# GpSimd takes VectorE's divisions and value rests between the halves of an attention stage, and the output projection is moved ahead of the value products

## The chip, the cores and the metric

One core of one Trainium2 chip runs the whole program. The metric is the device time of one execution in microseconds (us); lower is better. Three executions of the kernel before took 1723.38, 1724.31 and 1725.91 us, median 1724.31.

## The reference, cut to what matters

The program is a tower on x of shape (4, 64, 750): a token mixer that gives h of shape (4, 750, 192), a linear attention, a mixture of 8 experts (two per token), a softmax attention with relative positions, and a mixture of 8 experts (one per token). The change is in the softmax attention alone. Per batch element, with 12 heads of 64:

```python
q, k, v = split(x @ wq), split(x @ wk), split(x @ wv)     # (B, 12, 750, 64), x is the layernorm of h
attn = (einsum("bhid,bhjd->bhij", q, k) + einsum("bhid,ijd->bhij", q, rpk)) * 64 ** -0.5
attn = softmax(attn, axis=-1)
out = einsum("bhij,bhjd->bhid", attn, v) + einsum("bhij,ijd->bhid", attn, rpv)
h = h + (out.transpose(0, 2, 1, 3).reshape(B, N, 768) @ wproj + bproj)
```

rpk and rpv are sums of two table rows, one for the vertical and one for the horizontal distance of two places in a 27-wide grid. All is float32.

## The kernel before

**Tiling.** `window_attention` works through 4 batch elements of two halves each, a half being 6 heads (HG). The 750 tokens are 6 tiles of 125 (CH, P). Products run on fp32r operands that are split into a rounded part and a rest (hi and lo), so that a product is three matmuls: hi by hi, hi by lo and lo by hi. The rest is the full value less the rounded one and has to be formed by some engine.

**Words.** In `words` (L2236, L2453, L2769) a half runs 36 steps, one for each head and key tile: scores on TensorE (L2254), two exponentials on ScalarE (L2500: a_Phi rounded, a_PT full), the rest of the exponential on VectorE (L2803: a_Plo), and the value products on TensorE (L2266 to L2273). Eight steps ahead a row product (L2150) and a VectorE maximum (L2678) give each query's maximum, which is turned into a row (L2157, L2684: a_mrow) and laid by a DMA (L1882) into row 127 of a_qhi, so that the scores come out with it subtracted. GpSimd forms the queries' rests (L1970: a_qlo), two heads ahead, and does nothing else in this stage.

**Between two halves** stand, for the old half, the value tables (`value_tables`: TensorE L2100 and L2112, copied by ScalarE L2415 and added by VectorE L2666 into a_outs) and the division of a_outs by the softmax sums (VectorE L2671, three multiplications by a_rdens' copy in the memory of a_qhi), then the projection out; for the new half the query tables (`query_tables`, L2137 to L2144), whose rows ScalarE (L2427) and VectorE (L2726) copy into a_work, one half of the heads each, and then `boundary`. Every engine runs its own list in the order in which it is written, and they meet by counted semaphores:

- TensorE, `boundary` (L2160): the value products `token_values` (L2176, 6 tiles into the two banks of a_S1), the projection out `project_out` (L2192, 6 tiles into the two banks of a_O, one tile of 192 columns in each), the first eight row products `first_rows` (L2150) and `max_to_row` (L2157). `token_values(c)` waits for the rest of tile c-2, which reads the same bank.
- ScalarE, `boundary` (L2420): copies of the queries (L2388), the table rows (L2427), then by turns a head of a_qhi (L2438) and a tile of a_vhi (L2441). The first head waits for the division, whose divisor lies in a_qhi.
- VectorE, `boundary` (L2686): the table rows (L2726), then `update` (L2723, h plus the projected tile), `values_rest` (L2694, a_vlo from the bank and a_vhi), `first_maxima` (L2678) and `first_row` (L2684), by turns.

The first scores of the new half wait for the row DMA (L2247), for the queries' rest (L2246) and for the seventh maximum; the first value product waits for all six value rests (L2279). There are eight such boundaries: one at the entry (no old half), seven between halves; three of the seven end an iteration of a loop over the batch elements, and the last of these leaves the loop. After the last half the old half is divided and projected with no new one.

## Time and profile before

| | |
|---|---|
| median of 3 runs | 1724.31 us (1723.38 to 1725.91) |
| span of the profiled execution, first to last instruction | 1721.1 us |
| its own time beside the span | not listed; the median of the runs is 3.2 us above this span |
| TensorE busy | 1534.4 us, 89% |
| VectorE busy | 1190.8 us, 69% |
| ScalarE busy | 988.4 us, 57% |
| GpSimd busy | 341.2 us, 20% |
| softmax attention, entry boundary to last projection | about 420 to 1505 us |

Engines are PE (TensorE's matmuls), PEld (its weight loads), DVE (VectorE), ACT (ScalarE), POOL (GpSimd) and SPq (the queue from which SyncE issues DMAs). A matmul on plain float32 (L2137, L2192) is two records in the trace, one on fp32r (L2176, L2150) is one. A matmul's end is modelled and overlaps the next one; the starts of the weight loads give the pace.

### The profile page before, as it was taken

To read this page: it belongs to the slowest core of one execution; us is meant where nothing else is said; L and a number is where in the kernel's file an instruction comes from. 1 tells how busy PE (TensorE), PEld (TensorE's weight loads), DVE (VectorE), ACT (ScalarE), POOL (GpSimd) and SP (SyncE) were. 2 spreads that over 40 slices of the span, in tenths; PEclk is the share of its full clock that TensorE was granted. 3 is DMA by queue.
4 is the path that set the end of the run, shared out by engine and by line. 5 is a ranking of instruction groups with operands and counts; after the bars stand their busy time and mean duration, and the time that the engine had idled before them with its cause. 6 is when DMAs were issued, how large, how long until landed. Compare 5 with 4: busy or idle time off the path is not lost. (4 is left out here: it accounts for less than half of the span.)

```text
span 1721.1 us, 32129 instructions
## 1 busy us (share of the span) xinstructions
PE 1534.4 (89%) x10815; PEld 1409.8 (82%) x10816; DVE 1190.8 (69%) x2245; ACT 988.4 (57%) x1777; POOL 341.2 (20%) x499
## 2 busy tenths in 40 slices
PE   5983999937999999899999999999999999848997
PEld 5762999936898898899898899998989889737996
DVE  4887555549775786786787677678677678575443
ACT  5541222226677578578677667667757757562221
POOL 5131566640000000110100010000000010014443
PEclk9985999968999999999999999999999999958999
DMA  8212111164101101100110110110010111091221
GB/s 266 70 51 80 48 57 57 56 142 120 44 11 38 45 11 39 46 11 19 30 44 11 31 45 20 30 44 20 29 45 10 39 35 51 20 291 49 63 58 29
DMA packets 61936, 94.83 MB, mean 55 GB/s; under 512 B 15644, under 2 KB 46511, under 8 KB 61422
## 3 DMA queue, kind: packets, MB, share of 16 engines
q1 hardware_dynamic: 52606, 72.92, 14.7%
q0 software_dynamic: 9200, 20.21, 4.1%
q8 instruction: 78, 1.28, 0.3%
q14 instruction: 52, 0.43, 0.1%
HBM read 72.58 MB, written 21.06 MB: 54 GB/s over the span
## 5 line engine op out<-in xcount | busy, mean ns | idle before, releaser
L2678 DVE TENSOR_REDUCE a_nmx<-a_M 125x1 f32<-125x752 f32 x256 | 240.7, 940 | 129.7 <-PE a_M L2150 128.8
L2500 ACT ACTIVATE a_Phi<-a_S 125x756 fp32r<-125x756 f32 x288 | 231.0, 802 | 156.2 <-PE a_O L2273 146.5
L2803 DVE TENSOR_TENSOR a_Plo<-a_PT,a_Phi 125x756 fp32r<-125x756 f32 x288 | 280.9, 975 | 52.5 <-ACT a_PT L2500 51.7
L1970 POOL TENSOR_TENSOR a_qlo<-a_work,a_qhi 127x750 fp32r<-127x750 f32 x48 | 79.1, 1656 | 996.0 <-PE a_S L2254 509.3
L2500 ACT ACTIVATE a_PT<-a_S 125x756 f32<-125x756 f32 x288 | 230.0, 799 | 0.0
L2254 PE MATMUL a_S<-a_qhi,a_khi 128*125 128x378 f32 x576 | 155.4, 351 | 12.9 <-issue 6.1
L2266 PE MATMUL a_O<-a_Phi,a_vhi 125*128 125x378 f32 x576 | 150.3, 342 | 1.3 <-ACT a_PT L2500 1.3
L2273 PE MATMUL a_O<-a_Plo,a_vhi 125*128 125x378 f32 x576 | 147.5, 337 | 1.0 <-DVE a_Plo L2803 0.9
L2254 PE MATMUL a_S<-a_qhi,a_klo 128*125 128x378 f32 x576 | 146.9, 336 | 0.0
L2254 PE MATMUL a_S<-a_qlo,a_khi 128*125 128x378 f32 x576 | 146.9, 336 | 0.0
L2269 PE MATMUL a_O<-a_Phi,a_vlo 125*64 125x378 f32 x576 | 146.4, 336 | 0.0
L2150 PE MATMUL a_M<-a_khi,a_qhi 127*125 127x376 f32 x512 | 132.2, 339 | 0.4 <-DVE a_nmx L2678 0.4
L1215 PE MATMUL m_psY<-m_w,m_hidT 128*128 x696 | 130.0, 331 | 2.7 <-DVE m_hidT L1572 2.7
L1215 PEld LDWEIGHTS m_psY<-m_w,m_hidT 128*128 128x128 f32 x696 | 114.4, 190 | 9.5 <-issue 9.5
L2254 PEld LDWEIGHTS a_S<-a_qhi,a_khi 128*125 128x125 f32 x576 | 98.3, 187 | 26.4 <-issue 13.5
L2273 PEld LDWEIGHTS a_O<-a_Plo,a_vhi 125*128 125x128 f32 x576 | 104.1, 189 | 14.4 <-DVE a_Plo L2803 4.3
L1299 ACT ACTIVATE m_xT<-m_psX 128x128 fp32r<-128x128 f32 x85 | 23.6, 277 | 155.8 <-PE m_psX L1139 155.8
L1151 PE MATMUL m_psG<-m_w,m_xT 128*128 x540 | 110.9, 352 | 0.5 <-issue 0.4
L2266 PEld LDWEIGHTS a_O<-a_Phi,a_vhi 125*128 125x128 f32 x576 | 102.0, 190 | 11.1 <-issue 8.1
L2254 PEld LDWEIGHTS a_S<-a_qhi,a_klo 128*125 128x125 f32 x576 | 103.9, 187 | 0.0
L2254 PEld LDWEIGHTS a_S<-a_qlo,a_khi 128*125 128x125 f32 x576 | 103.8, 187 | 0.0
L1151 PEld LDWEIGHTS m_psG<-m_w,m_xT 128*128 128x128 f32 x540 | 93.7, 190 | 5.4 <-issue 3.2
(440 smaller groups left out, 3050.3 us busy)
## 6 DMA issues: line engine op xcount, KB each, us to landing
a_qhi<-a_rdens SPq DMA_DIRECT2D x48, 187.5 KB, 3.4
a_wkv<-a_w4k SPq DMA_DIRECT2D x8, 768.0 KB, 5.1
a_wq<-a_w4q SPq DMA_DIRECT2D x8, 768.0 KB, 6.6
a_wkv<-a_w4v SPq DMA_DIRECT2D x8, 768.0 KB, 5.6
m_w<-in_m_w SPq DMA_DIRECT2D x8, 576.0 KB, 9.3
m_X<-m_xn SPq DMA_DIRECT2D x8, 504.0 KB
m_w<-in_m_w SPq DMA_DIRECT2D x8, 384.0 KB, 6.2
m_w_ahead<-in_m_w SPq DMA_DIRECT2D x8, 384.0 KB, 8.1
```

The source lines that it names most:

```text
L1151: last = nc.tensor.matmul(psG[buf][:, g, 0:half], tokens, w1[0:rows_, bass.ds(e, 1), k, g * half:(g + 1) * half].rearrange("d o f -> d (o ...
L1215: last = nc.tensor.matmul(psY[:, 0:E], hidT[:, k * 128:(k + 1) * 128], w2[:, bass.ds(here, 1), k, :].rearrange("f o e -> f (o e)"), start= ...
L1299: nc.scalar.activation(xT[:, buf, 0, :], psX[:, 0:SLOT], ACT.Copy)
L1970: pool.tensor_tensor(qlo[0:ONE, u % HG % QLO, :], work[0:ONE, u % HG, 0:L], qhi[0:ONE, u % HG, :].bitcast(F32), ALU.subtract).then_inc(sg[ ...
L2150: last = nc.tensor.matmul(bank[0:P, a, 0:376], qhi[0:ONE, u % HG, c * P:(c + 1) * P], khi[0:ONE, u % HG, a * 374:a * 374 + 376], start=Tru ...
L2254: last = nc.tensor.matmul(psS[wd % 2][0:P, a, 0:HP], kk[:, u % HG, at], qq[:, PART[a]:PART[a] + HP], start=(x == 0), stop=(x == 2))
L2266: nc.tensor.matmul(psO[:, a, 0:HP], vhi[:, c, u % HG, :], Phi[:, wd % 2, at[a]], start=(c == 0), stop=False)
L2269: nc.tensor.matmul(psO[0:HD, a, 0:HP], vlo[:, c, u % HG, :], Phi[:, wd % 2, at[a]], start=False, stop=False)
L2273: last = nc.tensor.matmul(psO[:, a, 0:HP], vhi[:, c, u % HG, :], Plo[:, wd % 2, at[a]], start=False, stop=(c == CH - 1))
L2500: last = nc.scalar.activation(to[:, wd % 2, :].rearrange("p (a l) -> p a l", a=2), psS[wd % 2][0:P, :, 0:HP], ACT.Exp, scale=SCALE)
L2678: v.tensor_reduce(nmx[:, u % 2, c:c + 1], bank[0:P, :, 0:376], AX.XY, ALU.max, negate=True).then_inc(sg["max_ready"], 1)
L2803: v.tensor_tensor(Plo[:, wd % 2, :], PT[:, wd % 2, :], Phi[:, wd % 2, :].bitcast(F32), ALU.subtract).then_inc(sg["exp_rest"], 1)
```

## The change

- **Division.** The three multiplications of a boundary between halves go from VectorE to GpSimd, at the same point of the program. After the last half they stay on VectorE.
- **Value rests.** GpSimd forms a_vlo from a full copy of each value tile in SBUF (`vfull`, in the memory of a_pairs, five tiles deep), which ScalarE makes ahead of a_vhi. A bank of a_S1 is free once ScalarE has made both copies; VectorE no longer reads it.
- **Projection out.** Two tiles share a bank of a_O (384 columns), so 6 tiles are 3 groups. Groups 0 and 1 stand ahead of the value products, group 2 after the fourth row product. VectorE adds two tiles of h in one instruction.
- **ScalarE's order.** A head of a_qhi comes before value tiles 0, 2 and 4; heads 3, 4 and 5 come after all value tiles.
- **GpSimd's order.** Its list becomes: division, rest of head 0, value rests 0 and 1, rest of head 1, value rests 2 to 5, and, inside the words, the rests of heads 2 to 5.

```diff
+VF = 5
...
+        vfull = pairs[0:P].rearrange("p a l -> p (a l)")[:, 0:VF * HG * HD].rearrange("p (c e) -> p c e", c=VF)
...
-            "projected": 12,
-            "h_updated": 12,
+            "projected": 6,
+            "h_updated": 6,
...
-            with pool.Fori(0, B) as i:
+
+            def queries_rest(i, u):
+
                 wait = waiter(pool, i)
-                for half in range(2):
-                    for u in range(half * HG, half * HG + HG):
-
-                        wait("qhi_ready", u + 1)
-                        if u % HG >= QLO:
-                            wait("scores_ready", (u - QLO + 1) * CH)
-                        pool.tensor_tensor(qlo[0:ONE, u % HG % QLO, :], work[0:ONE, u % HG, 0:L],
-                                           qhi[0:ONE, u % HG, :].bitcast(F32), ALU.subtract
-                                           ).then_inc(sg["qlo_ready"], 1)
+                wait("qhi_ready", u + 1)
+                if u % HG >= QLO:
+                    wait("scores_ready", (u - QLO + 1) * CH)
+                pool.tensor_tensor(qlo[0:ONE, u % HG % QLO, :], work[0:ONE, u % HG, 0:L],
+                                   qhi[0:ONE, u % HG, :].bitcast(F32), ALU.subtract
+                                   ).then_inc(sg["qlo_ready"], 1)
+
+            def values_rest(i, half, c):
+
+                waiter(pool, i)("vhi_ready", half * CH + c + 1)
+                pool.tensor_tensor(vlo[:, c, :, :], vfull[:, c % VF, :].rearrange("p (h d) -> p h d", d=HD),
+                                   vhi[:, c, :, 0:64].bitcast(F32), ALU.subtract).then_inc(sg["vlo_ready"], 1)
+
+            def divide(i, half):
+
+                waiter(pool, i)("rel_h_added", (half + 1) * (NHS + 1))
+                pool.wait_ge(s_db, (2 * i + half + 1) * (32 * NPR))
+                for pr in range(NPR):
+                    pool.tensor_tensor(outs[:, pr, 0:L], outs[:, pr, 0:L], rdb[:, pr, :], ALU.mult
+                                       ).then_inc(sg["out_divided"], 1)
+
+            def boundary(i, half):
+
+                u0 = half * HG
+                queries_rest(i, u0)
+                values_rest(i, half, 0)
+                values_rest(i, half, 1)
+                queries_rest(i, u0 + 1)
+                for c in range(2, CH):
+                    values_rest(i, half, c)
+
+            def words(i, half):
+
+                for u in range(half * HG + QLO, half * HG + HG):
+                    queries_rest(i, u)
+
+            boundary(0, 0)
+            with pool.Fori(0, B - 1) as i:
+                words(i, 0)
+                divide(i, 0)
+                boundary(i, 1)
+                words(i, 1)
+                divide(i, 1)
+                boundary(i + 1, 0)
+            words(B - 1, 0)
+            divide(B - 1, 0)
+            boundary(B - 1, 1)
+            words(B - 1, 1)
...
                     else:
-                        wait("vlo_ready", half * CH + c - 1)
+                        wait("vhi_ready", half * CH + c - 1)
...
-                def project_out(c):
+                def project_out(g):
 
                     if old is None:
                         return
                     i, half = old
                     wait = waiter(pe, i)
-                    if c == 0:
+                    if g == 0:
                         pe.wait_ge(s_wp, 32 * i + 16 * (half + 1))
                         wait("out_divided", half * NPR + NPR)
-                    if c >= 2:
-                        wait("h_updated", half * CH + c - 1)
-                    for pr in range(NPR):
-                        last = nc.tensor.matmul(psO[0:P, c % 2, 0:E], outs[:, pr, c * P:(c + 1) * P],
-                                                wp[:, pr, :], start=(pr == 0), stop=(pr == NPR - 1))
+                    if g == 2:
+                        wait("h_updated", half * 3 + 1)
+                    for z in range(2):
+                        c = 2 * g + z
+                        for pr in range(NPR):
+                            last = nc.tensor.matmul(psO[0:P, g % 2, z * E:(z + 1) * E], outs[:, pr, c * P:(c + 1) * P],
+                                                    wp[:, pr, :], start=(pr == 0), stop=(pr == NPR - 1))
                     last.then_inc(sg["projected"], 1)
...
+                project_out(0)
+                project_out(1)
                 token_values(0)
                 token_values(1)
-                project_out(0)
-                project_out(1)
                 first_rows(0)
                 first_rows(1)
                 token_values(2)
+                first_rows(2)
+                token_values(3)
+                first_rows(3)
                 project_out(2)
-                first_rows(2)
-                first_rows(3)
-                token_values(3)
-                project_out(3)
                 first_rows(4)
                 first_rows(5)
+                token_values(4)
                 first_rows(6)
-                token_values(4)
-                project_out(4)
+                token_values(5)
                 first_rows(7)
-                token_values(5)
-                project_out(5)
...
-                for x in range(HG):
+                def head(x):
+
                     nc.scalar.activation(qhi[0:ONE, x, :], work[0:ONE, x, 0:L], ACT.Copy
                                          ).then_inc(sg["qhi_ready"], 1)
+
+                def values(x):
+
                     wait("v_product", half * CH + x + 1)
+                    if x >= VF:
+                        wait("vlo_ready", half * CH + x - VF + 1)
+                    nc.scalar.activation(vfull[:, x % VF, :], psS[1][0:P, x % 2, 0:HG * HD], ACT.Copy)
                     nc.scalar.activation(vhi[:, x, :, 0:64],
                                          psS[1][0:P, x % 2, 0:HG * HD].rearrange("p (h d) -> p h d", d=HD),
                                          ACT.Copy).then_inc(sg["vhi_ready"], 1)
+
+                for x in range(HG):
+                    if x % 2 == 0:
+                        head(x // 2)
+                    values(x)
...
+                for x in range(HG // 2, HG):
+                    head(x)
...
-                wait("rel_h_added", (half + 1) * (NHS + 1))
+
+            def divide(i, half):
+
+                waiter(dve, i)("rel_h_added", (half + 1) * (NHS + 1))
                 dve.wait_ge(s_db, (2 * i + half + 1) * (32 * NPR))
                 for pr in range(NPR):
...
-                def values_rest(c):
-
-                    if new is None:
-                        return
-                    i, half = new
-                    waiter(dve, i)("vhi_ready", half * CH + c + 1)
-                    v.tensor_tensor(vlo[:, c, :, :],
-                                    psS[1][0:P, c % 2, 0:HG * HD].rearrange("p (h d) -> p h d", d=HD),
-                                    vhi[:, c, :, 0:64].bitcast(F32), ALU.subtract).then_inc(sg["vlo_ready"], 1)
-
...
-                def update(c):
+                def update(g):
 
                     if old is None:
                         return
                     i, half = old
                     wait = waiter(dve, i)
-                    if c == 0:
+                    if g == 0:
                         dve.wait_ge(s_bp, i + 1)
-                    wait("projected", half * CH + c + 1)
+                    wait("projected", half * 3 + g + 1)
                     if half == 1:
-                        wait("h_updated", c + 1)
-                    hc = h[:, bass.ds(i * CH + c, 1), :].rearrange("p o e -> p (o e)")
-                    v.tensor_tensor(hc, hc, psO[0:P, c % 2, 0:E], ALU.add).then_inc(sg["h_updated"], 1)
+                        wait("h_updated", g + 1)
+                    hc = h[:, bass.ds(i * CH + 2 * g, 2), :]
+                    v.tensor_tensor(hc, hc, psO[0:P, g % 2, 0:2 * E].rearrange("p (c e) -> p c e", e=E), ALU.add
+                                    ).then_inc(sg["h_updated"], 1)
 
                 if new is not None:
                     relative_rows(dve, waiter(dve, new[0]), new[1], 1, lambda o, x: v.tensor_copy(o, x),
                                   "table_rows_dve")
                 update(0)
-                values_rest(0)
+                update(1)
                 first_maxima(0)
                 first_maxima(1)
-                values_rest(1)
-                update(1)
                 first_maxima(2)
                 first_maxima(3)
-                values_rest(2)
-                update(2)
                 first_maxima(4)
                 first_maxima(5)
-                values_rest(3)
                 first_row()
+                update(2)
                 first_maxima(6)
-                update(3)
                 first_maxima(7)
-                values_rest(4)
-                update(4)
-                values_rest(5)
-                update(5)
                 if old is not None:
-                    waiter(dve, old[0])("h_updated", (old[1] + 1) * CH)
+                    waiter(dve, old[0])("h_updated", (old[1] + 1) * 3)
...
                     inverse(i, 1, NPR - 1)
                     value_tables(i, 1)
+                    divide(i, 1)
                     dve.wait_ge(s_sd, 3)
```

TensorE's list at a boundary inside the loop, from the query tables' last product (a_M<-a_pairs,a_rqh) to the first row products. REGISTER_ALU and ISA rows prepare a wait. Before:

```order
L2144 MATMUL a_M<-a_pairs,a_rqh 64x3
L2169 REGISTER_ALU
L1845 REGISTER_ALU
L2176 MATMUL a_S<-a_wkv,a_hn 125x384 x5
L1845 REGISTER_ALU
L2176 MATMUL a_S<-a_wkv,a_hn 125x384 x5
L2187 REGISTER_ALU
L1845 ISA
L2192 MATMUL a_O<-a_wp,a_outs 125x192 x6
L1845 REGISTER_ALU
L2150 MATMUL a_S<-a_khi,a_qhi 125x376 x2
L2150 MATMUL a_M<-a_khi,a_qhi 125x376 x2
```

The same place in the changed kernel:

```order
L2188 MATMUL a_M<-a_pairs,a_rqh 64x3
L2231 REGISTER_ALU
L1848 ISA
L2238 MATMUL a_O<-a_wp,a_outs 125x192 x12
L2213 REGISTER_ALU
L1848 REGISTER_ALU
L2220 MATMUL a_S<-a_wkv,a_hn 125x384 x5
L1848 REGISTER_ALU
L2220 MATMUL a_S<-a_wkv,a_hn 125x384 x5
L1848 REGISTER_ALU
L2194 MATMUL a_S<-a_khi,a_qhi 125x376 x2
L2194 MATMUL a_M<-a_khi,a_qhi 125x376 x2
```

Four projected tiles instead of two now stand ahead of the first row product, and all four ahead of the value products.

ScalarE's list at the same boundary, from its second value tile to the first exponential of the words. Before:

```order
L2441 ACTIVATE a_vhi<-a_S 125x6x64
L2438 ACTIVATE a_qhi<-a_work 127x750
L2441 ACTIVATE a_vhi<-a_S 125x6x64
L2438 ACTIVATE a_qhi<-a_work 127x750
L2441 ACTIVATE a_vhi<-a_S 125x6x64
L2438 ACTIVATE a_qhi<-a_work 127x750
L2441 ACTIVATE a_vhi<-a_S 125x6x64
L1845 REGISTER_ALU
L2500 ACTIVATE a_Phi<-a_S 125x756
```

In the changed kernel, from its last two value tiles on:

```order
L2482 ACTIVATE a_qhi<-a_work 127x750
L2490 ACTIVATE a_pairs<-a_S 125x384
L2491 ACTIVATE a_vhi<-a_S 125x6x64
L2490 ACTIVATE a_pairs<-a_S 125x384
L2491 ACTIVATE a_vhi<-a_S 125x6x64
L2482 ACTIVATE a_qhi<-a_work 127x750 x3
L1848 REGISTER_ALU
L2557 ACTIVATE a_Phi<-a_S 125x756
```

Each value tile is now two instructions, and three heads stand between the last value tile and the first exponential, where none stood.

## Rows read from the trace of the kernel before

**Rows 1.** The page's span and TensorE's line: busy us, share, instructions.
```profile
span 1721.1 us, 32129 instructions
...
PE 1534.4 (89%) x10815; PEld 1409.8 (82%) x10816; DVE 1190.8 (69%) x2245; ACT 988.4 (57%) x1777; POOL 341.2 (20%) x499
```
**Rows 2.** Timeline from 820 us: start us, length us, instructions [idle before <- releaser].
```profile
820.72 2.64 DVE L2671 TENSOR_TENSOR a_outs<-a_outs,a_qhi 128x750 f32<-128x750 f32 x3
...
823.39 2.72 DVE L2726 COPY a_work<-a_S 29x486 f32<-29x486 f32 x4
...
824.85 1.20 PEld L2137 LDWEIGHTS a_S<-a_pairs,a_rqh 128*64 128x64 f32 x16 [1.18 <-ACT a_work L2427]
...
829.40 2.08 PE L2176 MATMUL a_S<-a_wkv,a_hn 128*125 128x384 f32 x10 [1.51 <-DVE a_work L2726]
...
831.01 0.83 ACT L2438 ACTIVATE a_qhi<-a_work 127x750 fp32r<-127x750 f32 x1 [2.01 <-issue]
```
**Rows 3.** Timeline of the same boundary, from its first row product to the exponential.
```profile
833.11 0.35 PEld L2150 LDWEIGHTS a_S<-a_khi,a_qhi 127*125 127x125 f32 x2
...
833.79 0.91 PEld L2176 LDWEIGHTS a_S<-a_wkv,a_hn 128*125 128x125 f32 x5
...
834.71 1.04 PEld L2192 LDWEIGHTS a_O<-a_wp,a_outs 128*125 128x125 f32 x6
...
841.15 0.27 DVE L2684 CAST a_mrow<-a_M 6x125 fp32r<-6x125 f32 x1
...
844.20 0.49 ACT L2441 ACTIVATE a_vhi<-a_S 125x384 fp32r<-125x384 f32 x1 [0.98 <-PE a_S L2176]
...
844.84 0.65 PE L2254 MATMUL a_S<-a_qhi,a_khi 128*125 128x378 f32 x2
...
846.22 0.80 ACT L2500 ACTIVATE a_Phi<-a_S 125x756 fp32r<-125x756 f32 x1 [1.53 <-PE a_S L2254]
```
**Rows 4.** GpSimd's lines: one of all queries' rests (duration min/median/max), one group.
```profile
L1970 POOL TENSOR_TENSOR a_qlo<-a_work,a_qhi x48: 1508/1654/1820, 423.8 to 1449.4; 127x750 fp32r<-127x750 f32 x48
...
L332 POOL TENSOR_TENSOR h<-h,hm 125x192 f32<-125x192 f32 x24 | 12.1, 506 | 38.5 <-DVE h L727 38.5
```
**Rows 5.** Timeline at the entry boundary: the row, the scores, ScalarE's table load.
```profile
432.13 0.27 DVE L2684 CAST a_mrow<-a_M 6x125 fp32r<-6x125 f32 x1
...
434.36 0.61 PE L2254 MATMUL a_S<-a_qhi,a_khi 128*125 128x378 f32 x2 [0.17 <-DMA a_qhi<-a_mrow]
434.73 1.28 ACT L2500 ACT_TABLE_LOAD   x1
```
**Rows 6.** Groups by form from 540 to 1500 us: ScalarE's copies (busy, mean ns).
```profile
L2438 ACT ACTIVATE a_qhi<-a_work 127x750 fp32r<-127x750 f32 x42 | 34.6, 824 | 10.7 <-issue 10.0 <-ACT a_work L2427 0.7
...
L2441 ACT ACTIVATE a_vhi<-a_S 125x384 fp32r<-125x384 f32 x42 | 20.4, 486 | 48.4 <-PE a_S L2176 48.4
```
**Rows 7.** Timeline at the two boundaries after which the loop jumps back.
```profile
710.66 1.28 ACT L2500 ACT_TABLE_LOAD   x1 [2.52 <-issue]
...
984.72 1.28 ACT L2500 ACT_TABLE_LOAD   x1 [2.22 <-issue]
```
**Rows 8.** Timeline: first value products at the boundaries of 958, 1095 and 1233 us.
```profile
967.20 2.08 PE L2176 MATMUL a_S<-a_wkv,a_hn 128*125 128x384 f32 x10 [0.92 <-DVE a_work L2726]
...
1103.50 2.08 PE L2176 MATMUL a_S<-a_wkv,a_hn 128*125 128x384 f32 x10 [0.99 <-DVE a_work L2726]
...
1241.77 2.07 PE L2176 MATMUL a_S<-a_wkv,a_hn 128*125 128x384 f32 x10 [0.45 <-DVE a_work L2726]
```
**Rows 9.** Windows: stretch, length, busy us of PE, PEld, DVE, ACT, POOL, granted clock, DMA.
```profile
552.00:555.00 3.00, 1.51 (x10) 1.33 (x9) 2.59 (x7) 1.12 (x4) 0.00 (x0) 1.00 0.00 0
555.00:558.00 3.00, 3.00 (x11) 3.00 (x10) 0.00 (x0) 2.84 (x5) 1.93 (x2) 0.50 0.01 3
```
**Rows 10.** Timeline of the boundary at 545 us: its division and its row.
```profile
544.87 2.64 DVE L2671 TENSOR_TENSOR a_outs<-a_outs,a_qhi 128x750 f32<-128x750 f32 x3
...
566.87 0.27 DVE L2684 CAST a_mrow<-a_M 6x125 fp32r<-6x125 f32 x1
```

More of the change, by code:

```diff
@@ L1779, in sem @@
             return keep.enter_context(nc.semaphore(f"a1_{n}"))
[L1781 removed]
+        (wq, wkv, wp, rqv, rqh, rv, bp, qhi, qlo, khi, klo, work, pairs, outs, turning, vhi, vlo, hn, PT, Phi, Plo, nb, rdb, dcol, oh, ohT, st, rstd, mv_, mean, nmx, mrow, vfull) = room.all
         psS = [ctx.enter_context(nc.psum_tensor(f"a1_S{i}", [128, 2, 512], F32)) for i in range(2)]
```

5 lines of the change are left out of this document (2 added, 3 removed).

## The prediction

> **What bounds the kernel now.** I read the page first: the profiled execution spans 1721.1 us, TensorE is busy for 89% of it and GpSimd for 20% [rows 1]. In the words TensorE has no idle time that the change touches, so what the change can be worth lies between the halves. There I read the timeline of one boundary, and compared the other six with it. I count from the start of its division, t = 0 at 820.72. VectorE divides for 2.64 us and only then copies table rows (823.39). TensorE waits twice for those rows: 1.18 us before its fifth set of tables, 1.51 us before the first value products at 829.40 [rows 2]. Without the waits nothing there would keep it. Then row products, value products and projected tiles alternate; the first row product starts at 833.11 (t 12.4), the copy of the row of maxima at 841.15 (t 20.4), the first scores at 844.84 (t 24.1), and the first exponential at 846.22 (t 25.5), for which ScalarE had been idle 1.53 us [rows 3]. The next scores need that exponential, so the start of the exponential is what sets the words in motion. The other boundaries inside an iteration repeat these intervals to 0.1 us, but for those named below.
>
> **The change, step by step, at one boundary.**
>
> *Division.* It leaves VectorE's list, 2.64 us. On GpSimd no division is in the trace; the nearest row is its two-input subtraction of almost the same size, 1.51 to 1.82 us, median 1.65 [rows 4]. I take 1.65, since the median row is also what GpSimd needed inside the boundaries; three are 4.95 us, ending at t 5.1 (bounds 4.6 and 5.6). GpSimd has nothing else to do then. TensorE wants the result at t 6.0 (next step) and ScalarE's first head later, so the cost is nothing, covered by the table products; if these were gone it would be 5.1 us on the path. The Trainium skill speaks against the move: GPSIMD Engine Reference, section 4.1, puts elementwise work on a tile on VectorE because GpSimd takes about twice as long with two inputs. The rows agree (1.65 against 2.64 / 3 = 0.88), and by that rule, read as a cost on the path, seven moves would lose seven times 2.3 us, 16 us; by the order of the waits they lose none.
>
> *Table rows.* VectorE copies them 2.6 us sooner. TensorE loses its 1.18 us wait and ends the tables at 829.40 - 1.51 - 1.18 = 826.71, t 6.0.
>
> *Projection ahead.* Four tiles now follow, at the pace of the loads about 1.0 us each (the 1.04 row), 4.0 in all, then two value products of 0.92 (833.79 to 834.71) [rows 3]: first row product at t 11.8, that is 0.6 us earlier than before, with two more tiles done.
>
> *Maxima.* From the first row product to the row's copy took 8.0 us before, mostly VectorE: six maxima, three rests, three updates. The rests are gone and the updates are fewer. But the third pair of tiles (2.0 us) now stands between the fourth and fifth row products, and VectorE idles behind it. Laying out both lists with the durations of the rows I get 8.1 us again: the row's copy at t 19.9 instead of 20.4. What was saved on VectorE is thus mostly a wait of VectorE. The row's way through the DMA to the scores takes 434.36 - 432.13 = 2.2 us [rows 5], so scores could start at t 22.1, 2.0 us earlier than before: TensorE no longer has value and projection work left in between, and the DMA becomes the wait there.
>
> *ScalarE.* Each value tile is copied twice, and a head takes 0.82, a tile 0.49 us [rows 6]. The last value product lands at about t 21.0, its two copies take 0.85, and three heads behind them 2.5: t 24.3. So the exponential starts at t 24.3 and not at 22.1 + 1.4 = 23.5, and ScalarE's own list ends the wait. Gain: 25.5 - 24.3 = 1.2, with the heads' overlap 1.25 us. Bounds: 2.0 if the heads overlapped fully, 0.6 if nothing of them does and TensorE is 0.4 late.
>
> *Value rests on GpSimd.* Between 0.506 us for 192 columns and 1.65 for 750 [rows 4] 384 columns come to about 0.9 us. The last one ends at t 22.8; the first value product stands behind the first scores, at 23.2 or later. Covered by 0.4 us; GpSimd's queue behind it (rest of head 2) is wanted some 25 us later.
>
> *Elsewhere.* The **entry boundary** has no division and no projection to move. There ScalarE began its exponential table load at 434.73 right behind its list [rows 5]; with six more copies and three heads at the end that list ends 1.0 us later: +1.0 (bounds 0 and 2.5, the three heads). Where the **loop jumps back**, the table load stands too, and began 2.52 and 2.22 us after ScalarE's last instruction [rows 7]. That instruction ended at t 24.0 (844.20 + 0.49 here) and will end at t 24.4: +0.4 for each of the two (bound below -1.0, if the jump is taken while the heads still run). After the **last half** six updates become three, and the last is longer by what 192 more columns take, +0.2.
>
> *Covers that go.* In three boundaries TensorE ran at the lower clock level (0.50 granted, 1.2 GHz) while it worked on the tables, and was late; VectorE's division hid it. The wait before the value products was 0.92, 0.99 and 0.45 us there instead of 1.51 [rows 8]. Without the division this comes out: 0.6 + 0.5 + 1.1 = +2.2 (bounds 0, if the clock does not fall there again, and 4). In the boundary at 545 us the clock fell to 0.50 after a stretch in which TensorE was busy for 1.51 of 3 us [rows 9], and the row came at 566.87 - 544.87 = 22.0 instead of 20.4 [rows 10]: a price of 1.6 us. That idle stretch goes, but a new one of about 1.5 us stands before the first scores. I set the two against each other: 0 (bounds -1.6 and, at all seven, +11).
>
> **The sum.** Five boundaries without a jump back, -6.25; entry +1.0; two jumps +0.8; lost covers +2.2; end +0.2: -2.1 us. The span would be 1719.0. The median of the three runs lies 3.2 above the span of the profiled execution, so the time is 1722.2. A measurement of this kernel can tell about 0.2%, 3.4 us, from no change; the forecast is inside that, on the fast side.
>
> **The rivals.**
>
> *The full gain.* The clock does not fall on the tables, the slow stretch at 545 goes, and the jump overlaps the heads: -2.1 - 2.2 - 1.6 - 2.8 = -8.7 at most, 1718 for about half of the extra. For it: three of the seven boundaries in the trace had no slow stretch at all. Against: what precedes the tables is not changed. Chance 0.22.
>
> *The clock falls at the start of the words (slower).* TensorE will wait about 1.5 us for the row's DMA and again for ScalarE's first exponential behind its heads, close together, much as in the half-idle stretch before 555 us [rows 9]. Each fall costs 1.6 us. From four of seven boundaries on the kernel is slower than before by over 0.2% (-2.1 + 6.4 = +4.3); at five it takes 1728. Against: at the two jumps TensorE already idled for 2 us there and its clock stayed. Chance 0.12.
>
> *The division comes late.* GpSimd and VectorE could hold each other up, each division waiting for one table copy of 0.68 us (2.72 for four): three of them end at t 7.0, 1.0 us behind TensorE's wish, seven times, and the time is 1729. Against: GpSimd's subtraction kept its 1.65 us beside VectorE's work on PSUM [rows 4]. The Trainium skill, GPSIMD Engine Reference, section 8, sees contention only with VectorE instructions of two SBUF inputs or a two-port mode; by it this rival falls, as the table copies read PSUM. Chance 0.06.
>
> *It does nothing of what it says.* ScalarE's tail eats all: heads that do not overlap and a later last value product bring the exponential to t 25.3, and five boundaries gain 1 us together instead of 6.25; the other terms stay: +3.2, 1727.5. Chance 0.08.
>
> **How the numbers follow.** Forecast 0.52 (1720 to 1724.5; 0.13 of it beyond 3.4 us of gain), full gain 0.22, slow clock 0.12, late division 0.06, no gain 0.08. Faster by over 0.2% (below 1720.9): 0.13 + 0.22 = 0.35. Slower by over 0.2% (above 1727.8): 0.12 + 0.06 = 0.18. Within: 0.39 + 0.08 = 0.47. The range takes in the forecast, the nearer part of the full gain and the case of no gain: 1717.5 to 1727.5.
>
> **What would show it.** In the changed trace: GpSimd's divisions about 1.65 us each and over before the projection starts; no wait of TensorE for VectorE's table rows; first row product 11.8 and row copy 19.9 us after the last addition of the value tables; scores released by the DMA; three heads directly before the first exponential, at t 24.3. I am wrong if the exponential starts before t 23.6 (the heads do not bind) or TensorE waits for a_outs, or if the granted clock is 0.50 at the start of the words.

## The result, and the profile after

The changed kernel takes 1728.16 us (median of 15 runs, 1722.41 to 1732.80), the kernel before on the same chip 1723.61 (15 runs, 1719.70 to 1727.25). The ratio is 1.0027, 95% interval 1.0016 to 1.0038: slower by 4.6 us. The forecast was 1722.2, with a range of 1717.5 to 1727.5; the result lies above it. The profiled execution took 1728.09 us. All medians of this document leave out two runs, one of div_only and one of the kernel before, that took about 1800 us in a slower state of the chip.

The page, against [rows 1]:

```profile
span 1726.3 us, 32159 instructions
...
PE 1545.0 (89%) x10815; PEld 1422.9 (82%) x10816; DVE 1149.6 (67%) x2152; ACT 1007.5 (58%) x1825; POOL 421.6 (24%) x568
```

VectorE has 41 us less to do, GpSimd 80 and ScalarE 19 more, as laid out. TensorE's number of matmuls is the same and its busy time 10.6 us longer: the same work at a lower clock.

The timeline of the boundary that [rows 2] and [rows 3] show of before. The last addition of the value tables ends at 822.95, so t = 0 is at 823.08:

```profile
822.22 3.51 PE L2181 MATMUL a_S<-a_pairs,a_rqv 128*64 128x81 f32 x48
...
823.13 4.73 POOL L1987 TENSOR_TENSOR a_outs<-a_outs,a_qhi 128x750 f32<-128x750 f32 x3 [51.00 <-DVE a_outs L2723]
...
831.24 4.17 PE L2238 MATMUL a_O<-a_wp,a_outs 128*125 128x192 f32 x24
...
836.98 0.51 PE L2194 MATMUL a_S<-a_khi,a_qhi 127*125 127x376 f32 x2
...
844.86 0.28 DVE L2744 CAST a_mrow<-a_M 6x125 fp32r<-6x125 f32 x1 [0.36 <-PE a_M L2201]
...
846.50 2.27 ACT L2482 ACTIVATE a_qhi<-a_work 127x750 fp32r<-127x750 f32 x3
...
847.06 0.61 PE L2297 MATMUL a_S<-a_qhi,a_khi 128*125 128x378 f32 x2 [1.00 <-DMA a_qhi<-a_mrow]
...
848.66 0.80 ACT L2557 ACTIVATE a_Phi<-a_S 125x756 fp32r<-125x756 f32 x1
```

The division is over at t 4.8, and both waits of TensorE for table rows are gone. But the projection starts at t 8.2 and not 6.0, the first row product at t 13.9 and not 11.8, and the exponential at t 25.6, where it was before (25.5). From t = 0 to the first row product TensorE waits for nobody; it is slow. Two windows of the same profile, one on the tables and one at the start of the words behind a loop jump (columns as in [rows 9]):

```profile
821.00:827.00 6.00, 6.00 (x86) 5.83 (x84) 3.56 (x7) 4.17 (x8) 3.87 (x3) 0.50 0.20 72
...
711.60:715.00 3.40, 3.40 (x13) 3.40 (x13) 0.00 (x0) 2.33 (x4) 0.00 (x0) 0.57 0.01 2
```

0.50 is the lower of the two clock levels, 1.2 GHz (0.57 is a window that holds a little of the higher one, too). In this profile it lies on the tables in all seven boundaries, and at the start of the words behind the entry and behind both loop jumps; before it lay on the tables in three boundaries, once inside a boundary [rows 9], and at no words' start. What TensorE did before the jump's 0.50:

```profile
710.77 0.71 PE L2297 MATMUL a_S<-a_qhi,a_khi 128*125 128x378 f32 x2 [3.13 <-issue]
```

It had been idle for 3.13 us ahead of the first scores; before, at the same place, for 1.79:

```profile
710.38 0.61 PE L2254 MATMUL a_S<-a_qhi,a_khi 128*125 128x378 f32 x2 [1.79 <-issue]
```

### The profile page after: what moved, and what is told of

Its sections match the earlier page's. It is cut to its first block and busy times, and to the rows that moved or that the text cites. A ratio compares the mean times of both kernels' runs of the same rounds, so it can differ in the third digit from the quotient of the medians.

```text
span 1726.3 us, 32159 instructions
## 1 busy us (share of the span) xinstructions
PE 1545.0 (89%) x10815; PEld 1422.9 (82%) x10816; DVE 1149.6 (67%) x2152; ACT 1007.5 (58%) x1825; POOL 421.6 (24%) x568
## 5 line engine op out<-in xcount | busy, mean ns | idle before, releaser
L1987 POOL TENSOR_TENSOR a_outs<-a_outs,a_qhi 128x750 f32<-128x750 f32 x21 | 33.0, 1602 | 364.7 <-DVE a_outs L2723 364.7
L1299 ACT ACTIVATE m_xT<-m_psX 128x128 fp32r<-128x128 f32 x85 | 23.6, 277 | 155.3 <-PE m_psX L1139 155.3
L2309 PEld LDWEIGHTS a_O<-a_Phi,a_vhi 125*128 125x128 f32 x576 | 102.2, 190 | 11.1 <-issue 8.1
```

Of the source, the lines that this page charges most:

```text
L1987: pool.tensor_tensor(outs[:, pr, 0:L], outs[:, pr, 0:L], rdb[:, pr, :], ALU.mult).then_inc(sg["out_divided"], 1)
L2309: nc.tensor.matmul(psO[:, a, 0:HP], vhi[:, c, u % HG, :], Phi[:, wd % 2, at[a]], start=(c == 0), stop=False)
```

## The experiments

All were timed against the kernel before on their own chip, whose medians were 1723.85 to 1724.30 us. "Boundary" is below from the last addition of the value tables to the first exponential, "words" from there to the next such addition.

### Which part costs it

**div_only:** the kernel before; the division stands in GpSimd's list as in the changed kernel, the rest is as before.

```diff
-                for pr in range(NPR):
-                    v.tensor_tensor(outs[:, pr, 0:L], outs[:, pr, 0:L], rdb[:, pr, :], ALU.mult
+            def divide(i, half):
...
+                for pr in range(NPR):
+                    pool.tensor_tensor(outs[:, pr, 0:L], outs[:, pr, 0:L], rdb[:, pr, :], ALU.mult
```

> The kernel before with only the three divisions of a boundary moved from VectorE to GpSimd. Theory A (the granted clock): VectorE's 2.64 us of division used to hide a slow stretch of TensorE at the boundary; without it TensorE does the table products at 1.2 GHz in most of the seven boundaries and nothing hides that, so this kernel shows 0.50 at the tables in 5 to 7 boundaries, its first row product comes 12.4 us or later after the last value table, and its time is 1724 to 1728 us, near the changed kernel. Theory B (ScalarE's added copies cost the time, the division is a gain): the first row product comes at 11.2 to 11.8 us, the time is 1716 to 1720 us. Theory C (the order of the projection cost it): as B.

**rests_only:** the kernel before with `vfull` and the rests on GpSimd.

```diff
-                values_rest(0)
...
+                    nc.scalar.activation(vfull[:, x % VF, :], psS[1][0:P, x % 2, 0:HG * HD], ACT.Copy)
```

> The kernel before with only the values' rests moved to GpSimd, and so with ScalarE's second copy of each value product (6 per boundary, some 0.5 us each). Theory A (the granted clock after the division has left VectorE): division and its cover stay, so the time is within 0.2% of before, 1721 to 1726 us. Theory B (ScalarE): six copies of 0.5 us push the heads, exponentials start 1 to 2 us later in each of eight boundaries, 1728 to 1735 us. Theory C (projection's order): within 0.2%, as A.

**proj_only:** the kernel before with TensorE's list at the boundary and VectorE's `update` as in the changed kernel; VectorE still forms the rests, the third and the fourth two maxima earlier than before.

```diff
+                project_out(0)
+                project_out(1)
                 token_values(0)
                 token_values(1)
-                project_out(0)
-                project_out(1)
```

> The kernel before with only the projection out changed: two tiles per bank, groups 0 and 1 ahead of the value products, VectorE adds them in three instructions instead of six; division and rests stay on VectorE. Theory A (clock): division and its cover stay; tables end at 7.2 us as before and four tiles in one piece then take 4.0 us, the first row product stays at 12.4 us within 1 us; 1720 to 1726 us. Theory B (ScalarE): as A. Theory C (the order): TensorE now stands behind VectorE's update and rests, the first row product comes 1.5 us later or more, 1728 us or more.

**after_dve_div:** the changed kernel, the division back on VectorE ahead of the table rows.

```diff
+                    v.tensor_tensor(outs[:, pr, 0:L], outs[:, pr, 0:L], rdb[:, pr, :], ALU.mult
...
-                divide(i, 0)
```

> The changed kernel with only the division back on VectorE, where it stood before (between the last relative sum and the table rows). Theory A (clock): the cover is back, the slow stretch at the tables is hidden again, but the order of the projection and the rests stay; time 1722 to 1726 us, lower than the changed kernel's by 2 to 5 us. Theory B (ScalarE) and theory C (order): the division was a gain and is now lost, so 1 to 1.2 us more in each of seven boundaries, 1730 to 1736 us.

**div_rests:** both moves to GpSimd, in the order of the kernel before. Against the changed kernel it lacks two things: the projection's new order, and ScalarE's three heads at the end of its list.

> The changed kernel's two moves to GpSimd (division and rests) in the order of the kernel before: projection one tile at a time, each behind a value product. Main theory (the projection's new order takes what the division gives): as the division alone plus the rests' cost, 1714 + 2 = 1716 us, 1713 to 1719; TensorE's clock falls at the tables in 5 of 7 boundaries or fewer, and nowhere at the first scores. Rival (division and rests compete on GpSimd, and only together cost anything): 1720 us or more, with TensorE or ScalarE waiting for vlo.

| | us, median | ratio to before, 95% |
|---|---|---|
| div_only | 1713.50 | 0.9941 (0.9925 to 0.9957) |
| rests_only | 1725.68 | 1.0015 (1.0003 to 1.0027) |
| proj_only | 1734.68 | 1.0063 (1.0047 to 1.0078) |
| div_rests | 1714.78 | 0.9950 (0.9935 to 0.9965) |
| after_dve_div | 1726.13 | 1.0019 (1.0005 to 1.0032) |

My first theory (A, the division's cover was what hid the clock, so its move is no gain) falls: the division's move alone gains 10.3 us, though the clock did fall on the tables in five of seven boundaries, as A had it. The rests cost 1.8 us or, on top of the division, nothing that can be told. The projection's new order costs 10.8 us alone: **it is the largest of the parts that make the kernel slower**. The changed kernel takes 13.4 us more than div_rests, but not all of that is the projection's, since ScalarE's order differs too. heads_back, further down, is the changed kernel with ScalarE's old order: it takes 6.4 us less than the changed kernel and 7.0 more than div_rests, so both orders cost. The three parts alone add up to +2.3 of the 4.6 measured, without ScalarE's order, and what they cost depends on the others. proj_only's timeline, t = 0 at 822.55:

```profile
822.55 2.64 DVE L2670 TENSOR_TENSOR a_outs<-a_outs,a_qhi 128x750 f32<-128x750 f32 x3
...
830.68 4.17 PE L2194 MATMUL a_O<-a_wp,a_outs 128*125 128x192 f32 x24
...
836.42 0.51 PE L2150 MATMUL a_S<-a_khi,a_qhi 127*125 127x376 f32 x2
...
845.26 0.28 DVE L2683 CAST a_mrow<-a_M 6x125 fp32r<-6x125 f32 x1 [0.36 <-PE a_M L2157]
...
849.11 0.80 ACT L2499 ACTIVATE a_Phi<-a_S 125x756 fp32r<-125x756 f32 x1 [2.49 <-PE a_S L2253]
```

The first row product comes at t 13.9, behind four tiles, and the row's copy 8.8 us later, VectorE having the rests as well. The exponential comes at t 26.6, 1.1 us later than before, and at t 29.6 at both jumps, about 2 us later. All seven boundaries of this profile have 0.50 on the tables. They took 7.5 us more than the mean of three profiles of before, the words of the first seven halves 5.2 us more, and the way to the entry's first exponential 1.4 us less: this is where the 10.8 us are. At both jumps stood 3.4 to 3.5 us of idle time, and 0.50 with it. div_only's timeline in the boundary whose t = 0 is 816.64:

```profile
816.68 4.74 POOL L1978 TENSOR_TENSOR a_outs<-a_outs,a_qhi 128x750 f32<-128x750 f32 x3 [50.13 <-DVE a_outs L2697]
...
826.49 0.65 PE L2181 MATMUL a_S<-a_khi,a_qhi 127*125 127x376 f32 x2
...
839.58 0.80 ACT L2531 ACTIVATE a_Phi<-a_S 125x756 fp32r<-125x756 f32 x1 [1.53 <-PE a_S L2285]
```

First row product at t 9.9, exponential at 22.9: 2.6 us earlier than before, the whole division. That was a boundary at full clock; in the five of seven with 0.50 on the tables the first row product came at 11.1 to 11.9, which is still ahead of 12.4. In after_dve_div the division's place no longer mattered where the clock was at 0.50: the first row product came at 13.2 to 13.9, as in the changed kernel. In its two boundaries at full clock it came at 12.8 and 12.9, 1.0 us later than the changed kernel's 11.8. So in the slow boundaries, which are most, TensorE's own work with four tiles ahead of the row product is the chain, and VectorE's 2.64 us is hidden behind it.

### How much is chance: each kernel three times

> The kernel before once more, for a second profile. If its boundary hides TensorE's 1.2 GHz, the first row product comes 12.3 to 12.4 us after the last value table in every boundary whose 0.50 lies at the tables, and behind no jump is there 0.50; the halves' words take 108.4 to 108.9 and 112.2 to 112.8 us.

> The kernel before a third time, for the same count: 0.50 at the tables in 3 to 6 boundaries, the first row product at 12.3 to 12.4 us in them all, none behind a jump.

> The changed kernel once more, for a second profile. If the 0.50 stretches follow from the order of its work, the two behind the loop jumps (at 711 and 988 us) and the one behind the entry (438 us) are there again; at the table products of the seven boundaries 4 to 7 are there again, and the time follows their number: 1728 us if all are, 2 us less for each that is missing.

> The changed kernel a third time: 0.50 behind both jumps again, at the tables in 5 to 7 boundaries; first row product at 11.8 us without it and 13.2 to 13.9 us with it.

They took 1722.55 and 1724.11 us (before), 1724.15 and 1729.61 (changed). 0.50 on the tables is chance, to a good part: it was there in 3, 3 and 7 of seven boundaries before, in 7, 5 and 6 of the changed kernel. Whether 18 of 21 is really more than 13 of 21, three profiles each can't tell. What surely differs is what it does. The third profile of before at t = 0.0 to 3.0, with the clock at 0.50, and its first row product:

```profile
820.00:823.00 3.00, 3.00 (x48) 3.00 (x45) 2.97 (x4) 1.47 (x3) 0.00 (x0) 0.50 0.02 6
```

```profile
828.65 2.08 PE L2176 MATMUL a_S<-a_wkv,a_hn 128*125 128x384 f32 x10 [0.57 <-DVE a_work L2726]
...
832.38 0.65 PE L2150 MATMUL a_S<-a_khi,a_qhi 127*125 127x376 f32 x2
```

t 12.4 from 819.96, as at full clock: the slow tables only shorten the wait, to 0.57 from 1.51 [rows 2]. In all 13 such boundaries of before it is 12.3 to 12.4. The second profile of the changed kernel had two boundaries at full clock; this one has t = 0 at 546.24:

```profile
558.03 0.51 PE L2194 MATMUL a_S<-a_khi,a_qhi 127*125 127x376 f32 x2
...
565.92 0.28 DVE L2744 CAST a_mrow<-a_M 6x125 fp32r<-6x125 f32 x1 [0.36 <-PE a_M L2201]
...
568.12 0.61 PE L2297 MATMUL a_S<-a_qhi,a_khi 128*125 128x378 f32 x2 [0.99 <-DMA a_qhi<-a_mrow]
...
569.72 0.80 ACT L2557 ACTIVATE a_Phi<-a_S 125x756 fp32r<-125x756 f32 x1
```

First row product at t 11.8, copy of the row 19.7, scores 21.9, exponential 23.5: 2.0 us better than before. Only 3 of 21 boundaries were like this; in the other 18 the row product came at 13.2 to 13.9 and the exponential, where no loop jump stands ahead of it, at 24.8 to 25.6.

The 0.50 behind the two loop jumps is not chance: there in 6 of 6 cases of the changed kernel, in none of 6 before. That behind the entry was there in two of three, before in none. The one inside the boundary at 545 [rows 9] was there in two of three before and in none of the changed kernel. Means of the three profiles each, in us:

| stretch | before | changed | difference | forecast |
|---|---|---|---|---|
| first exponential of the entry, from the span's start | 435.7 | 436.7 | +0.9 | +1.0 |
| seven boundaries | 183.7 | 180.4 | -3.2 | -3.25 |
| words of the first seven halves | 773.0 | 777.8 | +4.8 | 0 |
| words of the last half | 102.6 | 103.6 | +1.1 | 0 |
| the rest | 226.5 | 227.0 | +0.5 | +0.2 |

4.0 of the 4.8 us stand in three halves: those behind the entry (+1.8) and behind the jumps (+1.0 and +1.2). The way to the entry's exponential differs by up to 1.6 us between profiles of one kernel, so its +0.9 is not sharp.

### What brings the clock down at the words' start

**group2_last:** the changed kernel; TensorE's third pair of tiles behind the last row product and the last value tile, which change places, and its update on VectorE behind the last maximum.

```diff
                 first_rows(3)
-                project_out(2)
...
                 first_rows(6)
-                token_values(5)
                 first_rows(7)
+                token_values(5)
+                project_out(2)
```

> The changed kernel with one edit: the projection's third pair of tiles stands behind the last first row product instead of between the fourth and the fifth. Theory idle (a long idle stretch of TensorE ahead of the first scores brings the 1.2 GHz at the words' start): 2.1 us of TensorE work fill the wait of 1.0 us (3.1 us at the loop jumps), 0.50 is gone from the words' starts, the first row's maxima end up to 2 us earlier and the first scores too, 1720 to 1724 us. Theory ahead (four tiles ahead of the first row product are the cost, since they and the slow tables are one chain): group 2 is not on it, only 0 to 1 us per boundary comes back, 1722 to 1728 us, and clocks stay. Rival: no change, 1728 us.

**heads_back:** the changed kernel; ScalarE's heads between the value copies.

```diff
-                    if x % 2 == 0:
-                        head(x // 2)
+                    head(x)
                     values(x)
...
-                for x in range(HG // 2, HG):
-                    head(x)
```

> The changed kernel with ScalarE's six heads back between the value copies (one per copy, as before) instead of three of them at the end. Theory tail (the three heads at ScalarE's end hold the first exponential, and TensorE then idles 1.8 us at the words' start, where its clock falls): the first exponential comes 1.4 us behind the first scores at entry instead of 3.0, no 0.50 there, 1.0 to 1.5 us at entry and up to 0.2 in each boundary: 1724 to 1727 us. Rival (ScalarE is then late with the value copies, and the value products wait): the first row's maxima or first scores come later by up to 1 us, 1728 to 1734 us.

**both:** these two edits together.

> The changed kernel with both edits that gained alone: the third pair of tiles behind the last first row product, and ScalarE's heads back between the value copies. If the two idle stretches of TensorE are separate causes, the gains add: 1728 less 9 less 6 gives 1713 us, 1711 to 1716, and no 0.50 at any words' start. Rival (both take away the same thing, or ScalarE's order then delays the values): 1717 to 1722 us.

**fill:** the changed kernel with matmuls behind the last row product whose results nobody reads.

```diff
+                    n = 5 if old is None else (7 if new[1] == 0 else 2)
+                    for x in range(n):
+                        nc.tensor.matmul(psO[0:P, 1, 0:376], qhi[0:ONE, 0, 0:P], khi[0:ONE, 0, 0:376],
```

> The changed kernel with matmuls that compute nothing that is used (into a bank of psO that is free) behind the boundary's last first row product: 2 at five of the boundaries and 5 at the entry, 7 at the two boundaries that end at a loop jump. Theory idle (TensorE's idle stretch ahead of the first scores is what brings 1.2 GHz at the words' start behind a jump): no 0.50 at the first scores behind either jump, the first scores themselves not earlier, and 1.2 to 1.4 us back in each of those two halves, 1723 to 1727 us. Rival (the 0.50 there comes with the order of the projection, not with the idle stretch): 0.50 stays at both jumps, and the added matmuls delay the scores by up to 2 us, 1728 to 1733 us.

**fill_jump:** the same with

```diff
+                    n = 14 if old is not None and new[1] == 0 else 0
```

> The changed kernel with 14 matmuls that compute nothing that is used behind the last first row product, at the two boundaries that end at a loop jump and nowhere else. With 7 of them TensorE was still idle for 2.11 and 2.46 us ahead of the first scores and the 0.50 came; 14 take some 2.7 us and leave under 1 us. Theory idle: no 0.50 behind the two jumps, 1.1 us back in each of the two halves, 1725 to 1727 us; first scores no later than 4.5 us behind the first row's cast. Rival (the order, not the idle time, brings it): 0.50 stays at both and the time is 1727 to 1731 us.

| | us, median | ratio to before, 95% |
|---|---|---|
| group2_last | 1719.37 | 0.9977 (0.9959 to 0.9995) |
| heads_back | 1721.76 | 0.9987 (0.9974 to 0.9999) |
| both | 1716.52 | 0.9959 (0.9941 to 0.9976) |
| fill | 1727.90 | 1.0021 (1.0007 to 1.0034) |
| fill_jump | 1724.65 | 1.0000 (0.9989 to 1.0010) |

fill looked like its rival: 0.50 stayed at both jumps, against what was expected. But TensorE had still been idle for 2.11 and 2.46 us ahead of the scores. fill_jump left 1.12 us:

```profile
705.01 2.55 PE L2283 MATMUL a_O<-a_khi,a_qhi 127*125 127x376 f32 x14
708.68 0.61 PE L2304 MATMUL a_S<-a_qhi,a_khi 128*125 128x378 f32 x2 [1.12 <-issue]
```

```profile
708.70:712.00 3.30, 3.11 (x16) 2.79 (x17) 0.59 (x1) 2.53 (x4) 0.00 (x0) 1.00 0.03 7
```

The clock stays at 1.00 behind both jumps, and **work that computes nothing makes the kernel 3.5 us faster**, of which 2.2 were expected; the intervals of the two ratios do not meet. In its profile the halves behind the jumps took 109.0 and 108.8 us, 1.0 and 1.3 less than the changed kernel's mean; the rest of the 3.5 is not traced to the edit. Idle time ahead of the first scores is thus shown as the cause at the jumps. It sorts all the profiles: 21 idle stretches there of 0.8 to 1.8 us (both jumps of the kernel before three times, div_only, rests_only, div_rests, group2_last, spread, both, fill_jump, and one of rows_first) with no 0.50 behind them, 15 of 1.9 to 3.6 us (the changed kernel three times, after_dve_div, proj_only, heads_back, fill, and the other of rows_first) with 0.50 at each, in four of them already before the scores. The falls on the tables are of another kind: TensorE has no gap of over 0.15 us in the 8 us ahead of them, in both kernels; what brings those was not found.

group2_last does with real work what the filler does. Its boundary that ends at the first jump (t = 0 at 683.33, 0.50 on the tables):

```profile
703.68 0.28 DVE L2744 CAST a_mrow<-a_M 6x125 fp32r<-6x125 f32 x1 [0.36 <-PE a_M L2201]
...
705.40 2.11 PE L2238 MATMUL a_O<-a_wp,a_outs 128*125 128x192 f32 x12
...
708.40 0.60 PE L2297 MATMUL a_S<-a_qhi,a_khi 128*125 128x378 f32 x2 [0.89 <-issue]
```

The row's copy comes at t 20.4 instead of 21.2 to 21.8, since VectorE's maxima no longer wait for a pair of tiles, and the pair fills the wait ahead of the scores. That is worth 8.8 us, a little more than the 4 to 8 expected of it. Part of it may be chance: in its profile three of seven boundaries were at full clock on the tables, against 3 of 21 in the changed kernel. In its other four, at 0.50, the exponential came only 0.3 us earlier than in the changed kernel where there is no jump, and 1.1 and 1.6 us earlier than its mean at the two jumps.

At the entry the idle time is of another kind. In the changed kernel ScalarE's three heads end its list, the table load comes behind them, and TensorE waits again just after its first scores:

```profile
432.25 2.27 ACT L2482 ACTIVATE a_qhi<-a_work 127x750 fp32r<-127x750 f32 x3
432.86 0.61 PE L2297 MATMUL a_S<-a_qhi,a_khi 128*125 128x378 f32 x2 [1.05 <-DMA a_qhi<-a_mrow]
...
434.53 1.28 ACT L2557 ACT_TABLE_LOAD   x1
...
437.37 0.61 PE L2297 MATMUL a_S<-a_qhi,a_khi 128*125 128x378 f32 x2 [1.81 <-ACT a_PT L2557]
```

heads_back had waits of 1.07 and 0.65 us there, no 0.50, and took 6.4 us less, more than the 1 to 4 expected; its one profile shows 2.4 of them at the entry and the half behind it, and up to 0.2 in each boundary; the rest is not traced. The 0.50 at the entry was seen in five of the eight profiles with the three heads at the end and in none of the others. The second profile of the changed kernel and that of fill_jump had the same waits and kept their clock, so these waits alone do not bring it, and the cause at the entry is likely, not shown. The two edits together gain 11.6 of the 15.2 us that they gain apart and land at 1716.5, between their expectation (1711 to 1716) and its rival (1717 to 1722).

### Where to put the projection

**spread:** the changed kernel with the pairs where the single tiles stood: the first behind the second value tile, the second behind the fourth, the third at the end. The value tiles and VectorE's updates go along; ScalarE's three heads stay at the end.

```diff
-                project_out(0)
-                project_out(1)
                 token_values(0)
                 token_values(1)
+                project_out(0)
                 first_rows(0)
...
-                token_values(3)
                 first_rows(3)
-                project_out(2)
+                token_values(3)
+                project_out(1)
```

> The changed kernel with the pairs of tiles put where the single tiles stood before: group 0 behind the first two value products, group 1 behind the fourth, group 2 at the end. Division and rests stay on GpSimd. Theory ahead: one pair (2.0 us) fewer ahead of the first row product, which comes at 9.9 us at full clock and 11.9 us at 1.2 GHz instead of 11.8 and 13.9; 2 us in each of seven boundaries, 14 us, less what the last pair takes at the end (up to 1 us): 1714 to 1718 us. Rival (banks of two tiles and the later update are the cost, not the place): 1725 us or more.

**rows_first:** div_only with the first tile behind the first two row products and the second to fourth each some places later; on VectorE the updates follow, and the row's copy goes ahead of the fourth rest.

```diff
                 token_values(1)
-                project_out(0)
-                project_out(1)
                 first_rows(0)
                 first_rows(1)
+                project_out(0)
```

> The kernel before with the division on GpSimd and, opposite to the changed kernel, the projection moved back: the first two row products stand ahead of any projected tile, the six tiles between the later ones. Theory (what stands between the tables and the first row product is on the path, two tiles are 2 us): the first row product comes at 7.8 us at full clock and 9.9 us at 1.2 GHz, the first row is cast 1 to 2 us earlier, 1708 to 1713 us. Rival (TensorE has no idle time left in the boundary, so the tiles only come later and hold the first scores): 1713 to 1717 us.

spread took 1723.06 us (0.9994, 0.9977 to 1.0012), rows_first 1715.03 (0.9950, 0.9936 to 0.9965). spread lies between what its theory (1714 to 1718) and its rival (1725 or more) expected. Its first row product came at t 9.9 at full clock as expected, but the copy of the row only 8.8 to 9.0 us later, against 7.9 in the changed kernel and 8.0 in div_only: the place gave 2 us and 1 went back, where a value tile and a pair now stand together between the fourth and fifth row products and an update stands between the maxima. That these take it is read from the lists, not tested, and the three heads at ScalarE's end are still in it. In rows_first the first row product came at 8.3 to 10.8 and the row's copy 8.9 behind it: it lands on its rival. The fastest are div_only (1713.50 us, 14.7 below the changed kernel), div_rests, rows_first and both (1716.52); their intervals overlap.

## Why the prediction was wrong

- **Division on GpSimd:** right in length (4.95 forecast, 4.73 measured) and covered. Its gain was put at 1.18 us of wait, and the second wait (1.51) was given to the projection; div_only shows that the move alone takes the full 2.6 us off the path at full clock (0.5 to 1.3 us of the first row product at 0.50), since VectorE is earlier for both. I never costed the division without the projection, and so missed that the projection costs more than it gives.
- **First row product 11.8, copy of the row 19.9, scores 22.1:** 11.8, 19.7 and 21.9, in the 3 of 21 boundaries at full clock. The DMA releases the scores, as forecast.
- **ScalarE's tail, exponential at t 24.3:** mis-sized, 23.5 at full clock, and so before t 23.6, the text's own sign that the heads do not bind. The last value product landed at t 20.5 and not 21.0, and the three heads took 2.2 us and not 2.5. The heads hold the exponential by 0.2 us in the boundaries (1.6 us behind the scores, 1.4 in heads_back).
- **Lost covers, +2.2:** mis-sized. It was summed over the three boundaries whose clock had fallen in one profile; over three profiles 18 of 21 boundaries fell, at up to 2.1 us each. The errors of this term and of ScalarE's tail cancel, together with a third: the slow stretch inside the boundary at 545, set at 0 against a new one, was gone in all three profiles (-1.7 us on average there). Seven boundaries together changed by -3.2 us, the forecast was -3.25: that is luck.
- **Entry, +1.0:** +0.9, within a scatter of 1.6. **Two jumps, +0.8:** +0.2 between the table and the exponential; what they cost came behind it. **GpSimd's rests** did not hold TensorE more than before: its scores waited for a_qlo 6 times, 1.5 us together, against 10 times and 2.4 us.
- **The words, 0:** the step that failed. The text set the slow clock behind the idle stretch at 545, which would go, against a new idle stretch before the first scores, at 0 together, and so left the words unchanged; they took 5.9 us more in eight halves, 4.0 of it behind the entry and the two jumps, where TensorE had become idle for longer.
- **The rival "the clock falls at the start of the words"** (0.12, 1728 us) had the place, though at the jumps and the entry and not at the boundaries in general; that it had the time is in part luck. It asked for five falls of 1.6 us; there were two or three, of 1.0 to 1.2 us at the jumps, and the halves without one were 0.1 to 0.3 us longer, the last 1.1. What spoke against it was a wrong reading: TensorE's 2 us idle at the jumps with the clock kept was taken as proof for 3.1 to 3.4 us, while my own steps had moved a value tile and two projected ones, about 3 us of TensorE's work, away from that place.
- **The rule of the Trainium skill** (GPSIMD Engine Reference, 4.1) that elementwise work belongs on VectorE: GpSimd was slower as it says, 1.6 us against 0.88, and it cost nothing on the path: moved alone, the division gained 10.3 us.

Not settled: why the words without a fall at their start, and the last half, are longer by 0.1 to 1.1 us (in part the fall on the tables, which begins up to 3.6 us ahead of the last addition and then lies in what I call words); and how much of the changed kernel's 4.6 us is the projection's order and how much ScalarE's, since the profiles compared also differ in the clock falls that come by chance.

## What to carry to other kernels

Cost each part of a change alone before the sum: here one part gained 10.3 us and another lost more. Count the order of the lists as a part of its own: ScalarE's order was in none of the single parts, and giving it back gained 6.4 us. Work that stands in an engine's wait is not only hidden, it also bridges the wait; when it is moved ahead, look at what idle time is left behind, above all at a loop jump, and at what must then run at the lower clock. A wait of TensorE for another engine can be the cover of its own slow clock: take the frequency of slow stretches from several profiles, not from one.

## What the runs showed of the hardware

After 1.9 to 3.6 us of idle time at a loop jump TensorE's granted clock was at 0.50, 15 times of 15: in four already before the next work, in the others at the latest 1.5 us into it. After 0.8 to 1.8 us it was so not once in 21. Fourteen unused matmuls (2.55 us) in such a gap kept it at 1.00. This line holds for the jumps alone: inside the boundary at 545 of the kernel before, 0.50 came behind waits of 0.9 and 1.5 us in two of three profiles, and at the entry it came behind waits of 1.1 and 1.8 us in some profiles and not in others. The same program had 0.50 on its tables, with TensorE busy ahead of it, in 3 of 7 boundaries in two executions and in 7 of 7 in a third. GpSimd's 128x750 float32 multiplication of two inputs took 1.51 to 1.80 us beside VectorE's copies from PSUM, and its 125x384 subtraction 0.99 to 1.03 us.
